# Transposing the attention probabilities of a windowed-attention kernel in groups of 49 rows instead of pairs of groups

## What is computed

```python
win = y.reshape(B, nWh, 7, nWw, 7, C)...reshape(B * nW, N, C)          # N = 49
q, k, v = (win @ qkv_w.T)...
attn = softmax(einsum('bhnd,bhmd->bhnm', q, k) * scale + bias + mask)
out = einsum('bhnm,bhmd->bhnd', attn, v)...
out = out @ proj_w.T + proj_b
x = shortcut + out
x = x + gelu(ln(x) @ fc1_w.T + fc1_b) @ fc2_w.T + fc2_b
```

## Time and profile before

| | us |
|---|---|
| median of three runs | 4877.54 (4868.76 to 4878.87) |
| the profiled execution | 4880.38 |
| its span, first to last instruction | 4878.6 |
| PE busy in the span | 4590.0 (94%) |
| DVE busy | 3646.7 (75%) |
| ACT busy | 3537.4 (73%) |
| POOL busy | 2552.6 (52%) |

### The profile page before, as it was taken

How to read it: one execution, slowest core, us unless ns; L and a number is a source line. 1 busy time by engine, 2 the same in 40 slices (tenths; PEclk the granted TensorE clock), 3 DMA queues, 4 the chain that set the end, 5 groups by cost and what they waited for, 6 DMA issues and landing times.

```text
span 4878.6 us, 192818 instructions
## 1 busy us (share of the span) xinstructions
PE 4590.0 (94%) x71190; PEld 3230.5 (66%) x71190; DVE 3646.7 (75%) x7461; ACT 3537.4 (73%) x5899; POOL 2552.6 (52%) x3498
## 2 busy tenths in 40 slices
PE   8999996999999999999999999999999999999998
PEld 5666664666666666666666666666666666666665
DVE  4343435888888888888888888888888888888886
ACT  3344444778778777877877877877787787787786
POOL 4344433555555555555555555555555555555554
PEclk9999998999999999999999999999999999999999
DMA  4445441100000100100100000010010010000000
GB/s 134 153 145 158 144 136 39 28 26 27 26 26 26 28 26 26 28 27 26 28 27 26 27 28 27 26 28 26 26 28 27 26 28 27 27 27 26 26 26 24
DMA packets 298299, 218.70 MB, mean 45 GB/s; under 512 B 43247, under 2 KB 245486, under 8 KB 298158
## 3 DMA queue, kind: packets, MB, share of 16 engines
q1 hardware_dynamic: 294632, 215.41, 15.1%
q10 hardware_dynamic: 3526, 1.12, 0.1%
HBM read 110.78 MB, written 111.94 MB: 46 GB/s over the span
## 4 chain that ended last, share of the span: by engine, by line
PE 64%; DVE 19%; issue 11%; ACT 5%; DVEq 1%; POOL 0%; DMA 0%; ACTq 0%; POOLq 0%
DVE xn L1084 9%; PE bank L577 8%; PE bank L658 7%; PE bank L633 6%; PE bank L502 6%; PE bank L569 5%; DVE sc L1059 5%; PE bank L600 5%; PE bank L515 4%; PE bank L649 4%; PE bank L560 3%; PE bank L587 3%; DVE z L1084 3%; ACT L862 2%; PE bank L480 2%
## 5 line engine op out<-in xcount | busy, mean ns | idle before, releaser
L1084 DVE SCALAR_TENSOR_TENSOR xn<-x,lnp 98x128 f32<-98x128 f32 x1024 | 874.0, 912 | 3.7 <-POOL lnp L1154 3.7
L1218 POOL TENSOR_TENSOR res<-x,projb 98x512 f32<-98x512 f32 x256 | 325.8, 1273 | 1013.9 <-DVE x L1101 1013.9
L1236 POOL TENSOR_TENSOR sc<-sc,mx 128x784 f32<-128x784 f32 x512 | 788.6, 1540 | 57.2 <-DVE mx L1065 57.2
L658 PE MATMUL bank<-g,fc_sb 128*128 128x392 f32 x2048 | 784.6, 506 | 0.2
L1059 DVE TENSOR_TENSOR sc<-bank,shared 128x392 f32<-128x392 f32 x1024 | 529.7, 560 | 310.5 <-PE bank L587 310.5
L862 ACT ACTIVATE g<-bank,fc1b 128x392 f32<-128x392 f32 x1024 | 574.1, 586 | 125.8 <-PE bank L651 112.5
L649 PE MATMUL bank<-zt_hi,fc_hi 128*128 128x392 f32 x1024 | 453.8, 443 | 153.1 <-ACT g L862 147.7
L600 PE MATMUL bank<-ident_sb,sc 128*113 128x128 f32 x4096 | 530.9, 273 | 0.3 <-ACT shared L872 0.2
L1154 POOL TENSOR_TENSOR lnp<-st 98x8 f32<-98x8 f32 x777 | 145.8, 216 | 731.6 <-DVE st L927 728.0
L600 PEld LDWEIGHTS bank<-ident_sb,sc 128*113 128x113 f32 x4096 | 515.6, 177 | 3.0 <-ACT shared L872 0.7
L1065 DVE TENSOR_REDUCE mx<-sc 128x16 f32<-128x784 f32 x512 | 496.7, 970 | 18.4
(11 more groups left out here) (106 smaller groups left out, 9187.0 us busy)
## 6 DMA issues: line engine op xcount, KB each, us to landing
x<-x_scratch SPq DMA_DIRECT2D x768, 49.0 KB
out_x<-y SPq DMA_DIRECT2D x672, 49.0 KB
xc_even<-in_x SPq DMA_DIRECT2D x128, 196.0 KB
shared<-in_x SPq DMA_DIRECT2D x128, 196.0 KB
x_scratch<-xc_even SPq DMA_DIRECT2D x128, 196.0 KB
x_scratch<-shared SPq DMA_DIRECT2D x128, 196.0 KB
x<-x_scratch SPq DMA_DIRECT2D x256, 38.5 KB
out_x<-y SPq DMA_DIRECT2D x224, 38.5 KB
```

The lines of the kernel that those rows point to most:

```text
L658: mm = nc.tensor.matmul(RC[:, 0:ST], fc2[:, c, :], g[:, c], start=c == 0, stop=c == HC - 1)
L1084: ins = V.scalar_tensor_tensor(dst[:, p, :], src[:, p, :], lnp[:, 7, i, p:p + 1], lnp[:, 8, i, p:p + 1].to_broadcast([PT, C]), ALU.add, AL ...
L1236: P.tensor_tensor(out=s_r, in0=s_r, in1=m_r.to_broadcast([128, 2 * HEADS, N]), op=ALU.subtract).then_inc(sub_done, 1)
```

## The change

`probs_t(t, j)` now does two pairs in one call, j = 0 or 1. Each transpose takes one window's 49 rows (partitions 0 to 48 or 64 to 112) of one quad and pair, 113 columns, against the 49 x 49 corner of the identity that lies in the same partitions. Window 0 goes to `RB[0]`, window 1 to `RB[1]`, in turn. A call has 16 transposes instead of the 4 of one old call, a strip 32 instead of 16. The call waits for both banks before its first transpose and adds 1 to a new semaphore, `probs_begun`, for which nothing waits. `pt_out(t, j, v)` copies one window of two pairs, 8 x 49 columns that lie close together in the bank. The number of copies stays four.

```diff
-                wait(pe, b_out[j % 2], out0(t, 1 + j // 2) if j % 2 == 0 else 4 * t.n + j // 2)
-                for q in range(QUADS):
-                    mm = nc.tensor.transpose(RB[j % 2][0:VT, 128 * q:128 * q + 128],
-                                             sc[:, t.u, q, j].rearrange("p h m -> p (h m)")[:, 0:VT], ident[:])
-                mm.then_inc(b_full[j % 2], 1)
+                wait(pe, b_out[0], out0(t, 1 + j))
+                wait(pe, b_out[1], 4 * t.n + j)
+                pe.sem_inc(probs_begun, 1)
+                for k in range(2):
+                    for q in range(QUADS):
+                        col = N * (QUADS * k + q)
+                        for v in range(2):
+                            rows = slice(QROWS * v, QROWS * v + N)
+                            mm = nc.tensor.transpose(RB[v][0:VT, col:col + N],
+                                                     sc[rows, t.u, q, 2 * j + k].rearrange("p h m -> p (h m)")[:, 0:VT],
+                                                     ident[rows, rows])
+                            if k == 1 and q == QUADS - 1:
+                                mm.then_inc(b_full[v], 1)
...
-            def pt_out(t, j):
-                act.wait_ge(b_full[j % 2], full0(t, 1 + j // 2) + 1 if j % 2 == 0 else 4 * t.n + j // 2 + 1)
-
-                full_ = RB[j % 2][0:VT, :].rearrange("p (q v n) -> p q v n", q=QUADS, v=2)
-                nc.scalar.activation(pt[:, j], full_[:, :, :, 0:N],
-                                     ACT.Copy).then_inc(b_out[j % 2], 1)
+            def pt_out(t, j, v):
+                act.wait_ge(b_full[v], full0(t, 1 + j) + 1 if v == 0 else 4 * t.n + j + 1)
+                nc.scalar.activation(pt[:, 2 * j:2 * j + 2, :, v, :], RB[v][0:VT, 0:2 * QUADS * N].rearrange(
+                    "p (k q n) -> p k q n", k=2, q=QUADS), ACT.Copy).then_inc(b_out[v], 1)
```

More of the change, by code:

```diff
@@ L257, in program @@
         conv2_begun, vb_clear = sem("conv2_begun"), sem("vb_clear")
+        probs_begun = sem("probs_begun")
         conv1_ps, h1_sb, conv2_ps, h2_sb = sem("conv1_ps"), sem("h1_sb"), sem("conv2_ps"), sem("h2_sb")
@@ L692, in strips @@
                     probs_t(t1, 0)
-                    probs_t(t1, 1)
                 if t3.there():
@@ L696, in strips @@
                 if t1.there():
-                    probs_t(t1, 2)
-                    probs_t(t1, 3)
+                    probs_t(t1, 1)
                 if t3.there():
@@ L901, in strips @@
                 if t1.there():
-                    pt_out(t1, 0)
-                    pt_out(t1, 1)
+                    pt_out(t1, 0, 0)
+                    pt_out(t1, 0, 1)
                 if t3.there():
@@ L906, in strips @@
                 if t1.there():
-                    pt_out(t1, 2)
-                    pt_out(t1, 3)
+                    pt_out(t1, 1, 0)
+                    pt_out(t1, 1, 1)
                 if t.there() or t1.there():
```

## The result

The changed kernel takes 5187.19 us (5181.64 to 5191.44) against 4875.11 us for the kernel before: a ratio of 1.0637, 95% interval 1.0624 to 1.0650. The direction was forecast; the forecast was +146 us, the measurement is +312 us. The profiled execution is 5181.64 us, its span 5179.9 us.

The account below looks back on a forecast made before the run. The prediction took DVE's chain to `ot` to bound each strip, PE having 0.28 us of air. PE's part growing 0.85 us, less air, gave 0.57 x 256 = 146 us: 5023 us, range 4905 to 5490.

Parts of the forecast that it names:

- The air: PE waits for DVE's `ot` before the projection, 0.40 and 0.16 us in turn, mean 0.28; only growth beyond it costs.
- The change of shape: Switching between 128-row and 64-row groups: loads 0.27 us behind `hidden`'s last matmul, next load 0.13 behind the last transpose.
- rival 2: Changing shape between 128-row and 64-row groups costs nothing; PE's part grows 0.46 us, time 4924; chance 0.12.
- The pace: In the transpose groups, 113-column loads set the pace, two row groups side by side: 0.094 us a pair.
- rival 1: Two 64-row groups do not load side by side: a pair takes 0.19 to 0.21 us, time 5410 to 5490; chance 0.18.
- rival 3: Transpose loads are fast, 0.05 us a pair; PE's part grows 0.13 us, time 4878, no change; chance 0.08.
- the rule of 0.83 ns a column: A load's time goes by columns, not rows, at 0.83 ns each: 0.094 us for the transposes' 113 columns.
- The new wait: Second transpose group waits for both ACT copies of the first: loads at 2.31 us, open wait 0.42 us.
- The sum at full clock: PE's part grows 0.85 us a strip; less the air, mean 0.57, times 256 strips gives 146 us.
- I cost both at nothing: Step on the transposes' changed bank writes and fewer columns written, both taken to add no time.
- the range to 5490: Forecast range for the whole kernel, 4905 to 5490 us, kept wide to include rival 1 and rival 2.
- mine: The prediction's main case: transposes make PE's part longer than the air, 5023 us, own range 4960 to 5100; chance 0.58.

Follow-up runs that it names:

- e1: Kernel before with only the change's waits: old 128-row transposes, 8 a group into both banks in turn, both waits ahead of the group; 4959 us, ratio 1.018.
- e2: Kernel before with two of each call's four transposes done twice, 8 more a strip, no new wait or shape; 5019 us, ratio 1.030.
- e4: Kernel before with DVE making `ot` ahead of the norm of x instead of behind it; 4804 us, ratio 0.986.
- e7: Kernel before with half of the `fc1_lo` products of the MLP's first product left out; 4874 us, ratio 1.000.
- e6: Changed kernel with the two windows one behind the other, 8 transposes each, each half waiting only for its own bank; 5589 us, ratio 1.146.
- e9: e4 with each transpose over 113 rows and a 113 x 113 identity instead of 128 x 128; 4774 us, ratio 0.979.
- e3: Changed kernel with an extra 128 x 196 product in PE's wait in front of the second transpose group, result not read; 5026 us, ratio 1.032.
- e12: Changed kernel with a fill of the size of e3's, but earlier, ahead of `hidden(t3, 2)` where PE waits for `gelu`; 5090 us, ratio 1.044.
- e10: e4 with PE's first two `probs_t` moved ahead of `hidden(t3, 2)`; 4837 us, ratio 0.992.
- e11: e9 and e10 together, with ACT's first two copies also ahead of its third `gelu`; 4679 us, ratio 0.960.
- e5: Changed kernel with transposes of 64 rows and 64 identity columns instead of 49 by 49; 5041 us, ratio 1.033.

## Why the prediction was right and wrong

**The air.** Right. Forecast 0.28 us a strip, from the earlier trace rows. Growth of PE's part less growth of the strip gives 0.91 - 0.61 = 0.30 in the changed kernel, 0.30 in e1, 0.27 to 0.28 in e2; e4 gains 0.27 by taking it away; e7 shows that nothing is won on PE below it. Also right: L642 no longer waits (0.6 us for `ot` in the whole span) and DVE waits for the attention, 286.8 us:

```profile
DVE ot L1077 <- PE bank L621: 286.8, 254, 7.7
...
PE bank L607 <- ACT shared L877: 87.1, 256, 1.0
```

**The change of shape.** Right on the way in: loads 0.27 us behind L660's start, forecast 0.27. So rival 2 falls. On the way back it is 0.19 us from the last transpose to the next load, forecast 0.13.

**The pace.** Nearly right: a pair of transposes every 0.099 us, forecast 0.094 (a group takes 0.99 with one duration of 0.259, so (0.99 - 0.26) / 15 = 0.049 for one). The two row groups do load side by side: 0.099 is far from rival 1's 0.19 to 0.21 and from rival 3's 0.055, and both fall. They do so in full: where one row group loads alone, at the start and the end of a group in e6, a load takes 0.099 us too, and a load of 113 rows in e9 the same. The missing 0.005 us is in the rule of 0.83 ns a column, which the prediction took from durations and not from starts.

**The new wait.** Right: the second group's loads at 2.31 us behind L660, forecast 2.31. The open wait, from 0.27 us behind the second L660's start to those loads, is 2617.26 - 2616.88 = 0.38 us, forecast 0.42; PE itself idles for 0.34. L667 streams at about 3.37, forecast 3.31, so PE's part grew by 0.91, forecast 0.85. Where e1's forecast was off it was in the same step: there the copies were done at 2.04 us, where I had taken 2.15.

**The sum at full clock.** 0.61 us a strip and 156 us, forecast 0.57 and 146.

**What failed** is a term that the sum doesn't have, the granted clock. I read the clock of the kernel before as a fact about the kernel, and took every duration of the changed kernel at full clock. The step "the shape of writes to the banks changes, the number of columns written falls; I cost both at nothing" gives no reason for the nothing, and it was the place where the narrower transposes should have been asked about. With them the granted clock falls to half for 365 us, which costs 156 us by the count of strips and 161 by e3, as much as everything else. A stretch of it, PE's timeline in the changed kernel:

```profile
2580.57 0.33 PE L660 MATMUL bank<-zt_lo,fc_hi 128*128 128x392 f32 x1
2581.25 1.76 PE L607 MATMUL bank<-ident_sb,sc 49*113 49x49 f32 x16 [0.34 <-ACT shared L877]
2582.94 2.98 PE L667 MATMUL bank<-g,fc_sb 128*128 128x392 f32 x4
```

The half clock begins with the second group of narrow transposes: 1.76 us instead of 0.99, then 2.98 for L667, which took 1.58 in e3 at full clock. Most stretches begin there: of the 63 stretches of half clock after the first 800 us, 59 begin between 1 and 4 us after a strip's first narrow transpose, which is the stretch from the end of the first group to just behind the second. In e6 it is 157 of 161, in e12, whose stretches are fewer, 39 of 43, all of them in the last of these microseconds. That the range to 5490 held the time was luck: it reached so far for rival 1, whose mechanism isn't there. The case that came true, mine with the clock falling beside it, had no chance given to it.

## What to carry to other kernels

Read the air of the edited engine against the engine that it waits for before counting anything: a shorter part gains nothing below it (e7), a longer one costs all above it (e1, e2), and the gain lies in the other engine's order (e4). When an edit makes matmuls narrower or puts pauses beside them, look at the granted clock in windows of a few us, and try the same edit with wider matmuls or a fill; a clock row in tenths hides a loss of 3%. When a producer is moved earlier, move the engine that frees its banks along with it (e10 against e11).

## What the runs showed of the hardware that I had not expected

**The clock can fall with hardly a pause.** In the changed kernel and in e6 PE goes to its 1.2 GHz level for some us at a time, for 365 and 975 us, although it is busy for 94% and 96% of the span. Its longest regular wait, 0.57 us a strip for `gelu`, stands in the kernel before as well (0.59 us). The pause of 0.34 us in front of the second group isn't it, since e1 has 0.41 and keeps its clock. What brings it about is 32 transposes of 49 rows by 49 columns a strip where 16 of 128 by 128 had stood. What keeps it: 64 by 64 in the same number and pace (e5), or 0.49 us of a wide product right in front of the second group (e3); a product of the same size 3 us earlier brings back more than half of it, not all (e12). How the chip weighs rows, columns and place is open: no run changed the columns alone.

The Trainium skill (TensorE: Matmul & The Clock Gate, HAM oscillation) ties the fall to gaps in which PE stands still between bursts, and its advice is to close the gaps. e6 doesn't agree: no wait for the copies (0.5 us in all) and the clock falls most. The same page (Part 4: PE-mode transpose) says that a transpose in transpose mode doesn't count as PE being busy in the same way. These kernels agree only in part: with 16 transposes of 128 columns (before), 24 of them (e2) or 32 of 64 (e5) the clock stays, with 32 of 49 it falls.

**Pace of loads on a part of the rows.** Loads of 113 columns on one group of 49 rows follow each other at 0.099 us (e6, start and end of a group), and on the 113 rows of e9 and e11 at 0.099 to 0.100; e11's groups show it, (0.96 - 0.26) / 7. Two groups of rows in turn need 0.049 a load (after). So fewer rows make no load faster, and a second row group beside the first makes none slower:

```profile
2605.38 0.96 PE L600 MATMUL bank<-ident_sb,sc 113*113 113x113 f32 x8
```

In the changed kernel's trace L516 (L515 before), which the change doesn't touch, takes longer than the transposes' loads:

```profile
L516 PEld LDWEIGHTS bank<-w_sb,h 64*98 64x98 f32 x2048 | 192.1, 271 | 15.1 <-ACT h L802 4.1 <-issue 0.5
...
L607 PEld LDWEIGHTS bank<-ident_sb,sc 49*113 49x113 f32 x8192 | 480.7, 185 | 229.7 <-issue 229.5
```

98 columns, each the fourth element of a row, take 271 ns, and 113 columns close together 185 ns. And a pair of them takes 0.18 us, where a pair of the transposes' takes 0.099. Since sharing between the row groups is excluded by the latter, the spacing of L516's operand is the likeliest cause. It isn't shown: the one is a product and the other a transpose, and no run changed the spacing alone. The Trainium skill (SBUF — State Buffer, Specifications (TRN2)) says that memory is read in lines of 16 bytes and that a line wants at least two hits for full rate; every fourth float32 is one hit a line, and the row agrees with that.
